# A fused two-layer graph network on one core: new instruction orders in the gate slots, layer 1's three matmul steps moved ahead of the gates' second part, and the filter copy cut in twelve

## What is computed

```
h = relu(layernorm(x))
# layer 0
c = relu(bn1(conv1x1(h.T)));  c = bn2(conv17(c));  x_conv = relu(c + h.T).T
s = h @ w_se.T + b_se;  A = exp(-|s_n - s_m|^2) * adj
msg = relu(h @ w_msg.T + b_msg);  x_nmp = A @ msg
gi = [x_conv, x_nmp] @ w_ih.T + b_ih;  gh = h @ w_hh.T + b_hh
r, z = sigmoid(gi_r + gh_r), sigmoid(gi_z + gh_z);  n = tanh(gi_n + r * gh_n)
x = x + (1 - z) * n + z * h
# layer 1
h = relu(layernorm(x));  out = x + relu(h @ w[:d] + (adj @ h) @ w[d:] + bias)
```

## Time and profile before

| | |
|---|---|
| median of 3 runs | 2178.36 us (2175.8 to 2182.96) |
| the profiled execution's own time | 2182.43 us |
| its span, first to last instruction | 2180.6 us |
| mean granted TensorE clock | 0.98 |
| busy share: PE, DVE, ACT, POOL | 88%, 70%, 36%, 24% |
| convolution stage | about 100 to 624 us |
| gate stage | about 664 to 2181 us |

### The profile page before, as it was taken

The page is one execution under the profiler, slowest core; times in us unless marked ns, Lnnn a source line. Parts: engine busy times, 40 slices in busy tenths (PEclk is TensorE's granted clock), DMA queues, the critical chain, the costliest instruction groups (busy, mean ns, idle before and its releaser), DMA issues.

```text
span 2180.6 us, 37547 instructions
## 1 busy us (share of the span) xinstructions
PE 1926.0 (88%) x13018; PEld 1443.8 (66%) x13018; DVE 1523.0 (70%) x3224; ACT 777.7 (36%) x1455; POOL 516.7 (24%) x642
## 2 busy tenths in 40 slices
PE   2867989999957999999999999999999999999997
PEld 2555767754426777777777777777777777777774
DVE  3868878842236777777777777777777777777775
ACT  3734445532233333333333333333333333333332
POOL 1022111110022232232232222222222222222221
PEclk9989999999978999999999999999999999999999
DMA  2156565564242222222221222222221222222220
GB/s 92 69 198 216 176 229 192 199 252 182 102 164 85 76 84 64 78 81 64 79 80 64 80 79 64 82 77 64 86 73 64 85 75 64 86 73 64 86 74 15
DMA packets 161273, 224.40 MB, mean 103 GB/s; under 512 B 15687, under 2 KB 112702, under 8 KB 160318
## 3 DMA queue, kind: packets, MB, share of 16 engines
q1 hardware_dynamic: 161214, 223.62, 30.6%
HBM read 133.39 MB, written 90.18 MB: 103 GB/s over the span
## 4 chain that ended last, share of the span: by engine, by line
PE 43%; DVE 17%; ACT 4%; issue 4%; ACTq 0%; DVEq 0%; DMA 0%; POOL 0%; POOLq 0%
PE ps_rz L1235 17%; PE ps_l L1235 12%; PE ps_n L1235 8%; PE ps_b L1235 5%; DVE update L1424 4%; ACT tanh_rz L1390 2%; DVE nmp L1341 2%; DVE att L1281 2%; DVE msg L1319 2%; ACT nmp L1336 2%; DVE diff L1421 2%; PE ps_adj L1261 1%; DVE reset L1398 1%; DVE x L1428 1%; DVE stats_b L1431 1%
## 5 line engine op out<-in xcount | busy, mean ns | idle before, releaser
L826 PE MATMUL m_ps<-big 128*128 128x512 f16 (+1 forms) x1152 | 268.7, 376 | 5.6 <-DVE ysb L736 3.7
L1415 POOL TENSOR_TENSOR x_new<-xin,new 128x256 f32<-128x256 f32 x128 | 94.4, 738 | 721.9 <-ACT new L1408 721.9
L1235 PE MATMUL ps_rz<-w_ih,nmp 128*128 128x512 f32 x768 | 206.4, 404 | 12.1 <-DVE nmp L1341 11.9
L1235 PE MATMUL ps_rz<-w_ih,conv_t 128*128 128x512 f32 x768 | 209.2, 407 | 0.0
L1235 PE MATMUL ps_b<-att_s,msg 128*128 128x256 f32 x768 | 108.4, 291 | 99.1 <-DVE msg L1319 99.1
L1268 ACT ACTIVATE adj_t<-ps_adj 128x512 fp32r<-128x512 f32 x64 | 38.2, 597 | 426.2 <-PE ps_adj L1261 426.2
L1235 PE MATMUL ps_rz<-w_hh,ht 128*128 128x512 f16 x768 | 186.6, 379 | 0.9 <-DVE sum_n L1384 0.9
L826 PEld LDWEIGHTS m_ps<-big 128*128 128x128 f16 x1152 | 112.6, 98 | 110.2 <-DVE ysb L736 5.1
L1235 PE MATMUL ps_l<-w_l,h2t 128*128 128x512 f16 x768 | 179.4, 384 | 1.4 <-DVE h2t L1469 1.4
L1235 PEld LDWEIGHTS ps_b<-att_s,msg 128*128 128x128 f32 x768 | 95.5, 190 | 111.7 <-DVE msg L1319 111.7
L1235 PEld LDWEIGHTS ps_rz<-w_ih,nmp 128*128 128x128 f32 x768 | 134.7, 188 | 51.3 <-DVE nmp L1341 27.3
(11 more groups left out here) (211 smaller groups left out, 4014.3 us busy)
## 6 DMA issues: line engine op xcount, KB each, us to landing
xin<-in_x SPq DMA_DIRECT2D x128, 256.0 KB, 2.9
spectra<-ysb SPq DMA_DIRECT2D x96, 256.0 KB, 2.0
rows<-spectra SPq DMA_DIRECT2D x64, 384.0 KB, 3.5
x_normed<-xhat SPq DMA_DIRECT2D x64, 256.0 KB, 3.3
h_turned<-ht SPq DMA_DIRECT2D x64, 256.0 KB, 2.2
adj_in<-in_adj SPq DMA_DIRECT2D x64, 256.0 KB, 3.7
ht<-h_turned SPq DMA_DIRECT2D x64, 256.0 KB, 3.3
xhat<-x_normed SPq DMA_DIRECT2D x64, 256.0 KB, 2.9
```

What stands on the lines that cost most here:

```text
L826: last = pe.matmul(dest, x_, w_, start=n == 0, stop=n == 11, skip_group_check=True)
L1235: last = pe.matmul(dest, stationary(dl), moving(wl), start=start and n == 0, stop=stop and n == 2, **kw)
L1415: pool.tensor_tensor(x_new[:, i, :], xin[:, p, i, :], new[:, i, :], ALU.add).then_inc(S["x_new_done"], 1)
```

## The change

In the gate stage the orders on three engines change; no instruction is added or taken away there.

- PE: after `weighted` come `turn2`, `inverse`, `layer1` and then `gates_second` for i = 0, directly followed by `gates_first` for i = 1.
- DVE: `new_rows` is cut into `x1_rows` (diff, update, x) and `x1_stats` (statistics); `messages_low` stands between them. `passed_low` moves ahead of the sums of half 0.
- ACT: `gate_tanh` of half 1 moves ahead of `adj_split_high`, and `passed_high` ahead of `gate_tanh` of half 0.

In the convolution stage the one 6 MB store of filters becomes twelve stores, one per slot in the slots 0 to 11, each behind that slot's load of x; and the 23 `negate` steps move from POOL to ACT: in slots 1 to 11 at the end of ACT's slot, in the later part behind the ACT half of a unit's eviction, two units late.

The diff, cut to its core:

```diff
--- before.py
+++ after.py
...
+                def store_filters(u):
+
+                    lo = X1_AT + 8 * D * u
+                    sp.dma_start(wb_d[:, 8 * D * u:8 * D * (u + 1)], big[:, lo:lo + 8 * D]).then_inc(wb_stored, 16)
...
                 load_x(1)
-                sp.dma_start(wb_d, big[:, X1_AT:X1_AT + SET]).then_inc(wb_stored, 16)
                 for q in range(SLOTS):
                     if q + 2 < graphs:
                         load_x(q + 2)
+                    if q < HALF_UNITS:
+                        store_filters(q)
                     if q < graphs:
                         store_xhat(q)
                         store_h(q)
...
-                def negate(u):
-
-                    lo, of = NEG_AT + 4 * D * u, WA_AT + 4 * D * (2 * u + 1)
-                    pool.tensor_scalar(big[:, lo:lo + 4 * D], big[:, of:of + 4 * D], -1.0, 1.0, ALU.mult,
-                                       ALU.mult).then_inc(negated, 1)
-
                 layer_rstd(0)
                 for q in range(graphs - 1):
                     layer_rstd(q + 1)
-                    if 1 <= q < HALF_UNITS:
-                        negate(q)
-                for u in range(HALF_UNITS):
-                    pool.wait_ge(wb_loaded[u], 16)
-                    negate(u)
...
                     if f % GROUP == 0 and g == 1:
-                        act.wait_ge(wb_stored, 16)
+                        act.wait_ge(wb_stored, 16 * HALF_UNITS)
...
+
+                def negate(u):
+
+                    lo, of = NEG_AT + 4 * D * u, WA_AT + 4 * D * (2 * u + 1)
+                    act.activation(big[:, lo:lo + 4 * D], big[:, of:of + 4 * D], ACT.Copy,
+                                   scale=-1.0).then_inc(negated, 1)
...
-                for m in range(first - HALF_UNITS, len(MAIN)):
+                    if 1 <= q < HALF_UNITS:
+                        negate(q)
+                for u, m in enumerate(range(first - HALF_UNITS, len(MAIN))):
                     split_y(m)
+                    if 2 <= u < HALF_UNITS + 2:
+                        act.wait_ge(wb_loaded[u - 2], 16)
+                        negate(u - 2)
...
-        def new_rows(dve, t, p, i):
+        def x1_rows(dve, t, p, i):
...
+
+        def x1_stats(dve, t, p, i):
             ready(dve, "x1_done", t, i + 1, H)
             dve.bn_stats(stats_b[:, i, :], x1[:, p, i, :]).then_inc(S["stats2"], 1)
             ready(dve, "stats2", t, i + 1, H)
@@ -1573,11 +1581,10 @@
...
                 def slot(t, p, prev, cur, nxt):
-                    if cur:
-                        adj_split_high(act, t, p)
                     if prev:
                         gate_tanh(act, t - 1, 1 - p, 1)
                     if cur:
+                        adj_split_high(act, t, p)
                         exponential(act, t, p)
                     if prev:
                         new_tanh(act, t - 1, 1 - p, 1)
@@ -1589,11 +1596,11 @@
                         h2_split_high(act, t - 1, 1 - p)
                     if nxt:
                         conv_read(act, t + 1, 1 - p)
+                    if prev:
+                        passed_high(act, t - 1, 1 - p)
                     if cur:
                         gate_tanh(act, t, p, 0)
                         new_tanh(act, t, p, 0)
-                    if prev:
-                        passed_high(act, t - 1, 1 - p)
                     if nxt:
                         conv_split_high(act, t + 1, 1 - p)
 
@@ -1613,9 +1620,12 @@
                         attention(dve, t, p)
                         messages_add(dve, t, p)
                     if prev:
-                        new_rows(dve, t - 1, 1 - p, 1)
+                        x1_rows(dve, t - 1, 1 - p, 1)
                     if cur:
                         messages_low(dve, t, p)
+                    if prev:
+                        x1_stats(dve, t - 1, 1 - p, 1)
+                    if cur:
                         adj_split_low(dve, t, p)
                     if prev:
                         norm2(dve, t - 1, 1 - p)
@@ -1623,13 +1633,12 @@
                         weighted_low(dve, t, p)
                     if prev:
                         h2_split_low(dve, t - 1, 1 - p)
+                        passed_low(dve, t - 1, 1 - p)
                     if cur:
                         gate_sums(dve, t, p, 0)
                         gate_new(dve, t, p, 0)
-                    if prev:
-                        passed_low(dve, t - 1, 1 - p)
-                    if cur:
-                        new_rows(dve, t, p, 0)
+                        x1_rows(dve, t, p, 0)
+                        x1_stats(dve, t, p, 0)
                     if nxt:
                         conv_split_low(dve, t + 1, 1 - p)
                     if prev:
@@ -1649,15 +1658,14 @@
                         messages(pe, t, p)
                         gates_first(pe, t, p, 0)
                         weighted(pe, t, p)
+                    if prev:
+                        turn2(pe, t - 1, 1 - p, cur)
                     if nxt:
                         inverse(pe, t + 1, 1 - p)
                     if prev:
-                        turn2(pe, t - 1, 1 - p, cur)
+                        layer1(pe, t - 1, 1 - p)
                     if cur:
                         gates_second(pe, t, p, 0)
-                    if prev:
-                        layer1(pe, t - 1, 1 - p)
-                    if cur:
                         gates_first(pe, t, p, 1)
                     if prev:
                         neighbours(pe, t - 1, 1 - p)

```

## The result

The changed kernel takes **2200.91 us** (median of 4 runs, 2198.72 to 2203.22), the kernel before 2177.16 us beside it (4 runs). The ratio is 1.0104, with a 95% interval of 1.0082 to 1.0126: about 1% slower. I had forecast 2236 us with a range from 2208 to 2264. The sign was right, the size was not: the loss is 24 us and not 58, and the time lies 7 us under my range. The profiled run took 2203.22 us with a span of 2201.3, at a granted clock of 1.00 in the gate stage, as before.

What follows compares the result with a forecast made beforehand. PE bounds the kernel: its own work, about 21.2 us a slot, plus two waits. Gate stage +74 and convolution -18.5 make +55.5, giving 2238 from the profiled run or 2234 from the median; forecast 2236 us, range 2208 to 2264.

Steps and rivals of the forecast that it cites:

- The convolution, -18.5 us: Convolution stage: 10.7 us gained from the split store, 7.9 from normalising without POOL's negations; ends -8 and -20.
- The three new waits: PE in the gate slot: new waits at h2hat's turn (1.19 us), layer 1 (0.73) and half 1's first part (about 1.0).
- the product is earlier: PE's product in each gate slot: starts at +6.50 instead of +7.86, a gain of 1.36 us a slot.
- the turn behind the product: PE, h2hat's turn: product issued at +8.04, turn waits until +9.23, costing 1.19 us a slot.
- from the turn to layer 1, with the wait for nmp gone: PE: layer 1 waits for h2t, cost 0.73 us a slot; the vanished wait before the second part gains 0.36.
- layer 1, second part, up to the first part of half 1: PE: half 1's first part waits until DVE has read half 0's sums, costing about 1.0 us a slot.
- the turn's start at +9.23: PE, h2hat's turn: start summed from statistics at +6.36 through aggregate, POOL's steps and h2hat: 6.36 + 0.47 + 0.26 + 1.36 + 0.78.
- h2hat 1.36 after POOL's start: Chain to PE's turn: h2hat starts 1.36 us after POOL's root steps start, read from 1513.99 to 1515.35.
- what follows it on ACT, POOL and DVE moves by the same 0.80: Gate slot: everything behind the attention, including the blocked update, starts 0.80 us earlier, as the attention does.
- My lower end for the slot, +0.9 us: Gate stage: price of 0.9 us a slot (+56 us) if the chain gained 0.3 more than the rows give.
- Rival 3: Gate stage: waits overlap more than counted, a slot costs 0.3 to 0.6 us, 2188 us at 0.45; 6 in 100.
- Rival 1: Gate stage: update escapes POOL, ending 1.0 us earlier, slots come out even, convolution's gain stays, 2160 us; 5 in 100.

Runs made afterwards that it cites:

- statistics first again: Changed kernel with DVE's low messages put back behind the statistics: 2201.13 us in its one run.
- the square: Four kernels with ACT and DVE as changed except u's place: second part first, 2060.7 (inverse first), 2093.5 (turn first); layer 1 first, 2201.3, 2200.9 us.
- PE's old order: Changed kernel with inverse, turn, gates' second part, layer 1 on PE again, and passed_high and passed_low at their old places: 2060.68 us, ratio 0.9454.
- PE's new order alone: Kernel before with only the new PE order, and passed_high and passed_low ahead of the sums: 2276.08 us, ratio 1.0443.

## Why the prediction was wrong

**The convolution, -18.5 us: right.** Alone it gives 18.9 us, the wait for x and the normalising each as forecast.

**The three new waits: right in place and kind.** Turn 0.68 us of idle time, layer 1 0.64, the first part of half 1 0.88 (forecast: about 1.0, 0.6, and 0.8 to 0.9), the last one exactly the bare price that the first slot showed. The forecast from the turn's start on holds: 24.5 - 9.23 = 15.3 us to the end of the slot, measured 24.04 - 8.59 = 15.5 in the slot shown, of which layer 1 takes 0.12 more (2.14 us behind the turn's start, not 2.02).

The terms of the sum, from start to start in the slots shown, need one more row of the kernel before, the first part of half 1:

```profile
1522.54 1.46 PE L1235 MATMUL ps_rz<-w_hh,ht 128*128 128x512 f16 x6
```

| term, us a slot | forecast | measured |
|---|---|---|
| the product is earlier | -1.36 | -1.65 |
| the turn behind the product | +1.19 | 2.38 - 1.54 = +0.84 |
| from the turn to layer 1, with the wait for nmp gone | -0.36 + 0.73 = +0.37 | 2.14 - 1.65 = +0.49 |
| layer 1, second part, up to the first part of half 1 | +1.0 | 5.74 - 4.81 = +0.93 |
| sum | +1.2 | +0.61 (0.64 in the mean of 62 slots) |

**The step that failed: the turn's start at +9.23.** It was +8.59. In the sum for it, "h2hat 1.36 after POOL's start" is the term that was most mis-sized; it measured 1.01. I took the 1.36 us from the earlier trace rows, where POOL's first root step (0.55 us) lies beside DVE's low messages. The change itself takes the messages away from that place, so the duration that I carried over held a wait which the change removes. The experiment with the statistics first again brought the 0.55 back, at 0.549 us in the mean, with the rest of the program as changed, and the last slot of the kernel before, which has no messages, shows 0.20 us and 1.01 us. I had seen this kind of mutual holding for `update` and did not ask whether other rows of the chain had it.

The rest, 0.29 us, lies ahead of it. Of this, 0.20 is in the end of `update`, where "what follows it on ACT, POOL and DVE moves by the same 0.80" did not hold. `new` hangs on the tanh, which the forecast itself had 1.00 us earlier, and only the attention was kept at 0.80 by the exponential. The rows of `new`, of the kernel before and of the changed one:

```profile
1509.56 0.51 ACT L1408 ACTIVATE new<-pre_n,w_scale 128x256 f32<-128x256 f32 x1 [0.47 <-DVE pre_n L1401]
```
```profile
1511.40 0.51 ACT L1414 ACTIVATE new<-pre_n,w_scale 128x256 f32<-128x256 f32 x1
```

It starts at +2.88 and at +1.90, 0.98 us earlier. Behind it stands `x_new` on POOL, and behind that the attention's low half, which goes from +4.33 to +3.36 and takes 1.44 us in place of 1.47. `update` ends 0.29 us after that, as before: at +5.09 and not at +6.09, 1.00 us earlier. Another 0.09 to 0.12 come from the low messages, which start before `x` has ended (0.34 us after its start); I had given each the full length. They do not read `x`; that this is the reason was not tested.

Together 0.64 us at the turn, and in the mean 24.5 - 23.95 = 0.55 us a slot; 62 x 0.55 = 34 of the 35 us between 2236 and 2201.

**Bounds.** My lower end for the slot, +0.9 us, was reached by "0.3 more gained by the chain"; the gain at the product was in fact 0.29 larger (+6.21), and the cost at the turn 0.35 smaller, and I had let only one of them vary. Rival 3 named almost the size (0.3 to 0.6 a slot, 2188) for another reason, that waits overlap. In part they do: the square shows the wait at the turn worth 33 us alone and nothing where layer 1 waits behind it. But my sum had that in it, since it counted along the chain of starts. Rival 1's mechanism, `update` free of POOL, did not occur in the changed kernel (1.39 us); brought about on purpose, upon the kernel with PE's old order, it took `update` from 1.39 to 0.42 us and gave 14.5 us, since DVE then has the low half to do, 0.68 us (that this is all of the reason was not tested).

**What my forecast did not say** is that the edits are three changes of opposite sign: -19 us in the convolution, -99 us on ACT and DVE as they act in PE's old order, and +140 us for one swap on PE. That ACT's gain survives PE's new order and DVE's does not shows in the numbers too: PE's new order alone less the convolution's gain is 2276.1 - 18.9 = 2257.2; ACT's head on top gives 2201.1 (56 us, beside 58 in the old order), and DVE's move on top of that 2200.9.

## What to carry to other kernels

A duration read beside another engine's instruction is a property of that neighbourhood; when a change moves either of the two, look for a row of the same instruction without company before carrying the number over. Here the last slot of the kernel before had one. And two chains that leave one point need not move alike: `new`, which hangs on the tanh, moved by 0.98 us, the attention, which hangs on the exponential, by 0.80 in the forecast (0.83 in the rows). On an engine that runs in order, a step whose operand comes from a chain over two other engines must have independent work between it and its producer: here layer 1 ahead of the second part put dependent steps back to back and cost 2.2 us a slot, which no reordering ahead of it removed. Test edits of one commit apart: two of these three parts were worth 5% together and were buried under the third.

## What the runs showed of the hardware

- A small GpSimd instruction is held by a vector instruction too, not only the other way round. POOL's 128x2 addition takes 0.20 us beside DVE's low half of adj, which reads one operand from PSUM, and 0.55 us when it starts beside DVE's low half of the messages, whose two inputs lie in SBUF: in the row of before (1513.99 to 1514.54) it ends 0.06 us after that instruction. The means are 551 ns (53 times, before), 195 (53, changed), 549 (52, statistics first), 197 (57, PE's old order); in the last slot of before, without messages, it is 0.20 us. The Trainium skill, SBUF — State Buffer, section Who interferes with whom, says that a DVE instruction with two SBUF inputs and a GpSimd instruction that reads SBUF exclude each other and that issue order decides who is blocked; these runs agree for both directions (`update` started 0.36 us after POOL's instruction and was held, 1.40 us; POOL's step started 0.17 us after DVE's and was held, 0.55 us).
- A wait of PE of 0.2 us shows no idle time in the profile, since PE's ends are modelled; the distance from start to start shows it (0.70 against 0.90 us from the last group before the product to the product).
- A wait for `sum_n` without work in front cost 56.0 to 56.1 us over 64 in each kernel that had it, whatever else was changed.
